# A graph-attention kernel: edges found in column groups, empty rows by a matmul, eleven batches

## The reference

```python
h = max(layernorm(x), 0);  x = x + L0(h, adj, W, a);  h = max(layernorm(x), 0);  return x + L1(h, adj)

# L0: attention with 4 heads of 32
Wh = (h @ W).reshape(N, 4, 32)
e = s_src[:, None, :] + s_dst[None, :, :]              # per head, from Wh and a
e = where(e >= 0, e, 0.2 * e);  e = where(adj[:, :, None] > 0, e, -9e15)
return elu(einsum('ijh,jhd->ihd', softmax(e, axis=1), Wh))    # a row without edges gets the mean of Wh
# L1: maximum over the neighbours
out = max over j with adj != 0 of x[j];  0 for rows without neighbours
```

## Time and profile before

| what | value |
| --- | --- |
| median of three runs | 566.72 us (566.58 to 567.52) |
| profiled execution, span | 568.4 us |
| PE, DVE, ACT, POOL busy | 64%, 73%, 53%, 64% |
| mean granted TensorE clock | 0.777 |
| DMA | 97.59 MB, 172 GB/s over the span |
| chain that ended last, by engine | POOL 14%, DMA 12%, issue 5%, PE 4% (the second stage's) |

### The profile page before, as it was taken

The page is one execution under the profiler, slowest core; times in us unless marked ns, Lnnn a source line. Parts: engine busy times, 40 slices in busy tenths (PEclk is TensorE's granted clock), DMA queues, the critical chain, the costliest instruction groups (busy, mean ns, idle before and its releaser), DMA issues. The chain is left out here.

```text
span 568.4 us, 9640 instructions
## 1 busy us (share of the span) xinstructions
PE 366.3 (64%) x2583; PEld 272.3 (48%) x2598; DVE 414.2 (73%) x1683; ACT 302.0 (53%) x747; POOL 364.5 (64%) x390
## 2 busy tenths in 40 slices
PE   1955367696768784984927373387766676667763
PEld 1723234363536463642917372155544565545553
DVE  7998896989968998798686768365656565565562
ACT  1988356465666766762020223465656565565661
POOL 5944377175777575676768521577777777777771
PEclk9979587797968797887665776567788778787687
DMA  8999868977989899761222100112222222332321
GB/s 265 390 282 425 349 229 296 329 277 258 369 316 342 338 342 359 288 225 40 52 52 39 44 28 28 46 53 56 57 62 58 64 62 67 69 66 68 72 69 38
DMA packets 36776, 97.59 MB, mean 172 GB/s; under 512 B 6896, under 2 KB 23536, under 8 KB 28528
## 3 DMA queue, kind: packets, MB, share of 16 engines
q1 hardware_dynamic: 18272, 71.51, 32.7%
q0 software_dynamic: 9984, 21.11, 15.8%
q10 hardware_dynamic: 8464, 4.33, 2.8%
HBM read 90.49 MB, written 6.42 MB: 171 GB/s over the span
## 5 line engine op out<-in xcount | busy, mean ns | idle before, releaser
L662 POOL DMA_INDIRECT G<-wh_table,idx x156 | 160.3, 1028 | 83.7 <-issue 45.0
L1284 POOL DMA_INDIRECT G<-h_table,idx x156 | 148.0, 949 | 52.4 <-issue 40.3
L682 ACT ACTIVATE adjb<-adjf 128x2048 bf16<-128x2048 int32 x64 | 121.7, 1902 | 48.2 <-PE psf L783 36.6
L1366 DVE TENSOR_TENSOR_SCAN S<-Fl,S,psf 128x128 f32<-128x128 f32 x117 | 56.1, 480 | 72.5 <-PE psf L1329 64.5
L1329 PE MATMUL psf<-identf,G 128*128 128x128 f32 x156 | 59.4, 380 | 61.8 <-DMA G<-h_table,idx 61.0
L1308 ACT COPY Sb<-psf 128x128 f32<-128x128 f32 x156 | 41.6, 267 | 81.3 <-PE psf L1335 80.3
L1344 PE MATMUL psf<-Sb,OL 128*128 128x128 f32 x312 | 79.8, 347 | 0.0
L782 PE MATMUL psf<-adjb,packw 128*128 128x512 bf16 x241 | 73.3, 457 | 9.1 <-ACT adjb L682 5.8
L1329 PEld LDWEIGHTS psf<-identf,G 128*128 128x128 f32 x156 | 26.2, 168 | 91.5 <-DMA G<-h_table,idx 89.2
L884 PE MATMUL psf<-E,OQ 128*128 128x64 f32 (+2 forms) x312 | 47.9, 326 | 26.6 <-DVE E L1124 26.6
L1294 ACT ACTIVATE dg<-identb,keep 128x128 bf16<-128x128 bf16 x156 | 63.0, 404 | 2.8 <-PEq L446 2.8
(11 more groups left out here) (142 smaller groups left out, 649.6 us busy)
## 6 DMA issues: line engine op xcount, KB each, us to landing
adjf<-in_adj_dram SPq DMA_DIRECT2D x64, 1024.0 KB, 9.2
G<-wh_table,idx POOLq DMA_INDIRECT x156
G<-h_table,idx POOLq DMA_INDIRECT x156, 2.5
wh_table<-OQ ACTq DMA_DIRECT2D x8, 272.0 KB, 4.8
xsf<-in_x_dram SPq DMA_DIRECT2D x4, 512.0 KB, 7.2
out_dram<-rows_out SPq DMA_DIRECT2D x32, 64.0 KB
h_table<-h1b ACTq DMA_DIRECT2D x2, 384.0 KB, 3.2
h_table<-h1b ACTq DMA_DIRECT2D x2, 256.0 KB, 2.3
```

The costliest lines, as they stand in the source:

```text
L662: pool.indirect_dma_start(G[:, plan.at[k] + b, :], None, wh_table, bass.IndirectOffsetOnAxis(ap=idx[:, n:n + 1], axis=0)).then_inc(gathere ...
L682: nc.scalar.activation(adjb[:, t % 2, c:c + N // 2], adjt[:, m % NA, :], ACT.Copy, accum_out=rc[:, t, m % 2:m % 2 + 1]).then_inc(adj_bf, 1)
L1284: pool.indirect_dma_start(G1[:, n % NG, :], None, h1_table, bass.IndirectOffsetOnAxis(ap=idx[:, n:n + 1], axis=0)).then_inc(found[n % NG], 16)
L1366: V.tensor_tensor_scan(S[:, n % 5, :], Fl[:, n % 3, :], ps[:, 1 + n % 2, 0:P], start, ALU.mult, ALU.max).then_inc(scan_done, 1)
```

## The change

From tile 4 on a row's K edges are no longer the K largest of all its candidates. The columns are in 2 to 4 groups (word c belongs to group c mod GR), and each group gets its own 8 slots: K = 8*GR. Such a unit is `flat`: no choice among words is made, and one MAX8 over the 64 candidates of a group gives its edges. Since a group's slots may be partly empty, `extract` also writes how many slots each earlier group left over, and `edges` turns an edge's place in the row into a slot with one compare and one max for each further group. Rows without neighbours get the mean of Wh (and 1 in the denominator) by a matmul of a diagonal `dnone`, made by ACT, into the sum of PE. The elu is computed as max(h, 0) + (min(exp h, 1) - 1), with exp straight from h. The cuts of the batches change, which makes eleven.

```diff
     def unit(t):
         b = blocks.get(t, 5 if t < 10 else 4 if t < 18 else 3)
-        return (t, 0, 1, 24 if t < 4 else 16, 8 if t < 4 else 4, b)
+        K, GR = (24, 8) if t < 4 else (32, 4) if t < 6 else (24, 3) if t < 12 else (16, 2)
+        return (t, 0, 1, K, GR, b)
-    cuts = [1, 2, 4, 7, 11, 16, 22, 28, tiles]
+    cuts = [1, 2, 4, 6, 9, 12, 17, 23, 29, tiles]
...
+def flat(unit):
+    return unit[2] == 1 and unit[3] == 8 * unit[4]
...
+    def steps(self, k):
+        u = self.batches[min(k, self.nb - 1)][0]
+        return u[4] - 1 if flat(u) else 0
+    def wide(self, k):
+        return self.batches[min(k, self.nb - 1)][0][3] + 7 + self.steps(k)
...
-        TAKE = [2, 2, 3, 3, 3, 4, 5, 5]
+        TAKE = [2, 2, 3, 2, 3, 3, 3, 5, 5]
         TAKE += [T - 1 - sum(TAKE)]
...
# scalar
-                    act.wait_ge(elu_in, f)
-                    nc.scalar.activation(ex[:, 0:len(tl), :], mn[:, 0:len(tl), :], ACT.Exp).then_inc(elu_out, 1)
+                    act.wait_ge(hp_ready, f)
+                    nc.scalar.activation(ex[:, 0:len(tl), :], hp[:, 0:len(tl), :], ACT.Exp).then_inc(ex_ready, 1)
...
                 for j, t in enumerate(plan.tiles(k - 2)):
+                    if j == 0:
+                        act.wait_ge(none_ready, k - 2)
+                    if t >= 2:
+                        act.wait_ge(agg_done, t - 1)
+                    nc.scalar.activation(dnone[:, t % 2, :], ident[:, :], ACT.Copy, scale=none[:, t:t + 1]).then_inc(dnone_ready, 1)
                     act.wait_ge(agg_done, t + 1)
...
# tensor
                         last = nc.tensor.matmul(ps[:, 6 + t % 2, 0:D + H], OQ[:, b, :], G[:, b, 0:D + H],
-                                                start=(n == 0), stop=(n == len(blocks) - 1))
-                    last.then_inc(agg_done, 1)
+                                                start=(n == 0), stop=False)
+                    if t == 0:
+                        pe.wait_ge(mean_ready, 2)
+                    pe.wait_ge(dnone_ready, t + 1)
+                    nc.tensor.matmul(ps[:, 6 + t % 2, 0:D + H], dnone[:, t % 2, :], mwh[:, :], start=False, stop=True).then_inc(agg_done, 1)
...
# vector, extract
                     for u in range(nu):
-                        n = mark(V.max(Xk[:, u, 8 * q:8 * q + 8], cnd[:, u * K * BITS:(u + 1) * K * BITS]))
-                    if q < K // 8 - 1:
+                        c0, c1 = (u * K * BITS, (u + 1) * K * BITS) if not steps else ((u * K + 8 * q) * BITS, (u * K + 8 * q + 8) * BITS)
+                        n = mark(V.max(Xk[:, u, 8 * q:8 * q + 8], cnd[:, c0:c1]))
+                    if q < K // 8 - 1 and not steps:
...
+                if steps:
+                    cg = part[:, 0:nu * GR].rearrange("p (u g) -> p u g", u=nu)
+                    yield from apart(V.tensor_reduce(cg, vk.rearrange("p u (g m) -> p u g m", m=8), AX, ALU.add))
+                    for i in range(1, GR):
...
# vector, edges
+                    yield from apart(V.tensor_tensor(pos, sel[:, :, K + 7:K + 7 + steps], spread(kq[:, bl], S, steps), ALU.add))
+                    for i in range(steps):
+                        n = mark(V.scalar_tensor_tensor(out=pos[:, :, i], in0=pos[:, :, i], scalar=8.0 * (i + 1), in1=pos[:, :, i],
+                                                        op0=ALU.is_ge, op1=ALU.mult))
...
+                    for i in range(steps):
+                        yield from apart(V.tensor_tensor(slot_q[:, 0:S], slot, pos[:, :, i], ALU.max))
...
# vector, finish and finish_rest
-                yield from apart(V.tensor_reduce(none[:, g], rc[:, g, :], AX, ALU.add))
-                yield from apart(V.tensor_scalar(none[:, g], none[:, g], 0.0, None, ALU.is_equal))
...
-                yield from apart(V.tensor_scalar(den[:, 0:nt, :], ag[:, 0:nt, D:D + H], 0.5, None, ALU.max))
...
-                    n = mark(V.scalar_tensor_tensor(out=hp[:, j, :], in0=mwh[:, :], scalar=none[:, t:t + 1], in1=hp[:, j, :],
-                                                    op0=ALU.mult, op1=ALU.add))
...
-                V.tensor_scalar(mn[:, 0:nt, :], hp[:, 0:nt, :], 0.0, None, ALU.min).then_inc(elu_in, 1)
+                yield from apart(V.scalar_tensor_tensor(out=xs[:, g, :].rearrange("p t d -> p (t d)"), in0=hp[:, 0:nt, :].rearrange("p t d -> p (t d)"), scalar=0.0,
+                                                        in1=xs[:, g, :].rearrange("p t d -> p (t d)"), op0=ALU.max, op1=ALU.add))
...
-                yield from apart(V.scalar_tensor_tensor(out=flat(hp[:, 0:nt, :]), in0=flat(hp[:, 0:nt, :]), scalar=0.0, in1=flat(ex[:, 0:nt, :]),
-                                            op0=ALU.max, op1=ALU.add))
-                yield from apart(V.scalar_tensor_tensor(out=flat(xs[:, g, :]), in0=flat(hp[:, 0:nt, :]), scalar=-1.0, in1=flat(xs[:, g, :]),
-                                            op0=ALU.add, op1=ALU.add))
+                yield from apart(V.tensor_scalar(line(ex[:, 0:nt, :]), line(ex[:, 0:nt, :]), 1.0, -1.0, ALU.min, ALU.add))
+                yield from apart(V.tensor_tensor(line(xs[:, g, :]), line(ex[:, 0:nt, :]), line(xs[:, g, :]), ALU.add))
```

More of the change, by code:

```diff
@@ L452, in edge_attention @@
         U = max(len(b) for b in plan.batches)
-        XW = max(len(b) * (b[0][3] + MW) for b in plan.batches)
+        XW = max(len(b) * plan.wide(k) for k, b in enumerate(plan.batches))
         SK = max(sum(u[5] for u in b) * b[0][3] for b in plan.batches)
@@ L485, in edge_attention @@
         some = sbl("some", [P, U])
+        part = sbl("part", [P, max(len(b) * b[0][4] for b in plan.batches)])
+        place = sbl("place", [P, max(plan.size[k] * plan.steps(k) for k in range(plan.nb))])
+        slot_q = sbl("slot_q", [P, SIZE])
         ends = sbl("ends", [P, 2, U])
@@ L515, in edge_attention @@
         bias = sbl("bias", [P, T])
[L516 removed]
+        wx = OQ[:, 12:14, :].rearrange("p a b -> p (a b)")[:, 0:WX]
         abc = OQ[:, 8:10, :].rearrange("p a b -> p (a b)")
@@ L829, in _ @@
             for k in range(NBT + 2):
-                K = plan.batches[min(k, NBT - 1)][0][3]
+                K, W_ = plan.batches[min(k, NBT - 1)][0][3], plan.wide(k)
                 if k < NBT:
@@ L857, in _ @@
                             for part in range(3):
-                                last = nc.tensor.matmul(ps[:, 2, o * (K + MW):(o + 1) * (K + MW)], Rm[:, plan.at[k] + o, :],
-                                                        Xb[:, part, u * (K + MW):(u + 1) * (K + MW)],
+                                last = nc.tensor.matmul(ps[:, 2, o * W_:(o + 1) * W_], Rm[:, plan.at[k] + o, :],
+                                                        Xb[:, part, u * W_:(u + 1) * W_],
                                                         start=(part == 0), stop=(part == 2))
@@ L942, in _ @@
             V.tensor_reduce(wx[:, D + H:D + 2 * H], wa[:, :, 0, :], AX, ALU.add).then_inc(wx_ready, 1)
+            V.memset(mwh[:, D:D + H], 1.0).then_inc(mean_ready, 1)
             for c in range(4):
@@ L968, in take_words @@
                     dve.wait_ge(packed, t + 1)
-                    words = ps[:, t % 2, :].rearrange("p (m g f) -> p f g m", g=GR, f=F)
                     for g in range(GR):
-                        last = V.max(wd[:, at + g * 8:at + g * 8 + 8], words[:, r, g, :])
+                        last = V.max(wd[:, at + g * 8:at + g * 8 + 8], ps[:, t % 2, r + g * F:C:GR * F])
                         if g < GR - 1:
@@ L1030, in rows_of_edges @@
                 nu, K = len(batch), batch[0][3]
-                W_ = nu * (K + MW)
+                W_ = nu * plan.wide(k)
                 Xk = X[:, k % 2, 0:W_].rearrange("p (u w) -> p u w", u=nu)
@@ L1088, in edges @@
                 dve.wait_ge(sel_done, k + 1)
-                sel = ps[:, 2, 0:S * (K + MW)].rearrange("p (b w) -> p b w", b=S)
+                sel = ps[:, 2, 0:S * plan.wide(k)].rearrange("p (b w) -> p b w", b=S)
                 n = mark(V.tensor_copy(meta[:, bl, :], sel[:, :, K:K + 3]))
                 mark(V.tensor_copy(sq[:, at, :], sel[:, :, K + 3:K + 7]))
+                steps = plan.steps(k)
                 yield
@@ L1127, in maxima @@
             def maxima(k):
+                tl = plan.tiles(k)
+                if tl:
+                    g = slice(tl[0], tl[-1] + 1)
+                    yield from apart(V.tensor_reduce(none[:, g], rc[:, g, :], AX, ALU.add))
+                    V.tensor_scalar(none[:, g], none[:, g], 0.0, None, ALU.is_equal).then_inc(none_ready, 1)
                 batch = plan.batches[k]
```

55 lines of the change are left out of this document (33 added, 22 removed).

## The result

The changed kernel took 582.76 us (median of four runs, 580.53 to 585.50) where the kernel before took 567.12 on the same chips: the ratio is 1.0249, with a 95% interval of 1.0215 to 1.0283. By the ratio it is slower by 14 us; the two medians lie 15.6 us apart. The forecast was 578.8, a ratio of 1.0213.

A forecast was written before the change was run, and what follows sets the result against it. From 229 us on, POOL's gathers plus hand-over were taken as the kernel's clock. `edge_max` starting 12.1 us later, at 373.1, and lasting an unchanged 207.4 gave a span of 580.5; less 1.7, 578.8 us, range 564 to 588.

The forecast's parts named there:

- the last step: Whole kernel, span to time: the span of 568.4 lay 1.7 us above the runs' median, so 580.5 became 578.8 us.
- The second stage unchanged: `edge_max`: its 156 gathers, their order and its code stay as they are, so it takes 207.4 us again.
- DVE's savings hidden: First stage: DVE is relieved by some 20 us net, and little of it lies on the path.
- One batch more: First stage, batches 4 to 10 instead of 4 to 9: the same 106 gathers, but six hand-overs for five.
- The gathers' times: POOL, first gathers of batches 5 to 10: 161.7, 186.6, 214.3, 248.0, 281.7 and about 314 us.
- PE's part between an E2 and L1080: PE's blocks at 0.234 us, 2.0 a pack, 0.4 for row counts: 8.8 us for batch 5, 9.3 for batch 6.
- The hand-over: POOL between batches: rstd, ACT's h1b, OQ and exponentials, then multiplications, delay the next gather; 8.35 us before, none of it DVE.
- Rival A: First stage paced by PE and DVE, not the gathers' loop: `edge_max` starts at 362 or 355, the latter 561 us; chance 0.17.
- The matmul: Aggregation, PE and ACT: the matmul with its activation adds 0.35 us a tile, bounds 0.23 to 0.6; 4.2 for two six-tile aggregations.
- B: Iterations 7 and 8: the adjacency loads can't follow with five tiles taken in each; price 3 to 8, 584 us; chance 0.12.
- C: POOL's gathers: if DVE holds POOL up, relief shortens 97 gathers by 0.08 each, 7.8 us: 571 us; chance 0.08.
- D: Search: a row with over 8 edges in one column group would force the many times slower `general_path`; excluded for this seed.

## Why the prediction was right, and where not

*Sign and size.* Right: slower was given 0.78, and the measured 582.76 lies in the range. The forecast was 4 us low, and only 0.9 of them lie in the sum: it gave a span of 580.5, and the profiled one is 581.4. The other 3.1 come from the last step. The prediction took 1.7 us off the span, because the span of 568.4 lay above the median of the runs before. But in every run listed here, and so in the profiled one after (583.04 us for 581.4), the time is 1.5 to 2.0 us longer than the span; the profiled execution before was a long one. That the span came out so well is in part luck: the exponentials of the last hand-over came 1.0 us late, the stretch to `edge_max` was 0.6 longer, and the second stage 0.8 shorter. The steps:

*The second stage unchanged*: 207.4 predicted, 206.6 measured.

*DVE's savings hidden*: right, and shown three times. The new cuts alone give nearly the same first gathers with the long search, the new search on the same eleven batches without the matmul is no faster, and ten batches with search and matmul give nothing. The estimate of DVE's net relief (some 20 us) was right too: 19.6 by the page. It went into L1080's waits: 35.1 us, where the kernel before has 4.7, the batches alone give 16.8, and batches and search 26.8. I expected 2 to 5 us for each; they were 5.94, 6.39, 3.72, 1.56, 6.16 and 11.32, the last because batch 10 has only three tiles to search while PE has 19 blocks of batch 8 to turn into rows and 20 of batch 7 to sum, most of it at the lower clock.

*One batch more*: right, and the largest term: 11.8 us by the cuts alone, 12.0 from ten to eleven, 13.4 from eleven to twelve (9.9, 12.0 and 10.9 by the ratios).

*The gathers' times*: batches 5 to 10 were predicted at 161.7, 186.6, 214.3, 248.0, 281.7 and about 314, and came at 163.38, 190.00, 217.06, 250.40, 284.19 and 314.98. POOL's idle before batch 5 was to be 8.7 and was 9.05. The mis-sized term is PE's part between an E2 and L1080: 8.8 and 9.3 us predicted for batches 5 and 6, 10.4 (141.34 to 151.74) and 10.9 (167.79 to 178.65) measured. I took a block's pair of L884 at 0.234 from a single row, at a granted clock of 1.00. In the first of these rounds the clock was 0.67 (141.4 to 146.5 us) and a pair took 0.35:

```profile
141.40 5.22 PE L905 MATMUL psf<-E,OQ 128*128 128x96 f32 x30 [1.82 <-DVE E L1178]
```

In the second it was 0.65 from 167.8 to 172.2 us. So the term was mis-sized by PE's clock: the sum priced the blocks of these rounds at the upper level.

From batch 7 on, the steps of 33.7 and 33.7 us were predicted, and 33.3 and 33.8 measured.

*The hand-over*: 8.1 us from the last gather of batch 8 (it ends at 276.09) to the first of batch 9 (284.19), where the earlier trace rows had 8.35, again with ACT in its middle. But the step by which, from 229 us on, this loop "is the clock of the kernel" fails. Taking ACT's h1b out of the hand-over moved the gathers and not the time, on either kernel. Rival A had the right second loop (PE and DVE) but made it too short: it had E2 of batch 9 end at some 305, and it ended at 317.2, and at 313.9 with the exponentials first. Its other price was also mis-summed, since three groups of 36 matmuls at 0.117 for 0.22 us would give 11 us and not 7; the lower clock stayed in the tail (0.50 in L905 at 317 and at 340 us). The mark of that second loop in the profile after is the 0.93 us of waiting for idx at 314.98. In the sum this did no harm, since both loops are about equally long and both were carried along to batch 7.

*The matmul*: 0.35 us a tile predicted with bounds of 0.23 and 0.6; 0.46 measured (1.15 less 0.69). The reason to take a value near the low end, that the activation overlaps the tile's own blocks, was wrong: ACT issues it after a copy for which it has waited for PE. In two groups of six tiles this makes 5.5 us for the 4.2 of the sum (an estimate; from the first to the last copy the two groups take 4.8 us longer than before). From the last exponential that POOL waited for ahead of the last gathers to `edge_max`, 62.8 was predicted and 63.4 measured.

*Rivals.* B: ACT waited 2.01 and 1.26 us for adjf from 237 to 243 us, but h1b at 245.12 then still waited 0.23 for POOL, so this cost next to nothing. C: the 106 gathers took 112.1 us with 30.5 of issue, 1.35 us each where they took 1.33:

```profile
L677 POOL DMA_INDIRECT G<-wh_table,idx x106 | 112.1, 1057 | 50.7 <-issue 30.5 <-DVE idx L1167 20.2
```

They did not get shorter though DVE was relieved by 20 us. The rule of the Trainium skill ("SBUF — State Buffer", section "SBUF: two separate sides"), by which POOL's descriptor writing is locked out while DVE is in a two-port mode, thus priced nothing here: the operations that the change removes were not what lengthened the gathers. No run here shows which were. D didn't occur.

*Open.* Moving the exponentials or offsets forward lengthened the stretch from the last batch's first gather to `edge_max` (59.8 us after, 61.6 with the exponentials first, 61.4 with both, and 62.3 for 60.5 on the kernel before); what in the tail takes it back was not found. A version with nine batches was not run, so whether one batch fewer would gain is open.

## What to carry to other kernels

In a pipeline written out by hand over engines that work in order, a further iteration has a price (here 10 to 13 us) though the work stays the same, because a round that passes from engine to engine hardly shrinks with its batch. A cheaper step inside pays only if it stands in the loop that closes last; before cutting work on the busiest engine, follow one whole round from a product to the same product of the next batch, over all engines. Where two loops are about equally long, an edit to one moves waits and no time, and an early wait on an in-order engine delays all that is queued behind it. Work moved to an engine for which the relieved one already waits can be a loss, the more so if it adds a hand-over for each tile (here some 2 us, within the noise). And a time is forecast from times: a span and a median of other executions don't give the offset between the two.

## What the runs showed of the hardware

No two indirect gathers of 128 rows started closer than 1.24 us in the first stage of any run (0.94 and 0.30 of issue), beside `adj`'s loads of some 300 GB/s or without them. The handing to and fro between PE and ACT for one tile, a pair of fp32 matmuls of 128x132 (0.49 us in most rows of the tail), a copy (0.27) and an activation of 128x128 (0.40), closed in 1.15 us in ten of the twelve steps of the tail and in 1.76 in the other two; in the 1.15, ACT spent 0.58 waiting. With the activation out of the circle it was 0.90 in eight of these twelve steps. PE's fp32 matmuls of 128x64 took 0.117 us each at a granted clock of 1.00 (40 in 4.68) and 0.22 at 0.50 (38 in 8.37). MAX8 over 64 columns took 0.135 us of the engine (7.8 us for 58), as the 0.142 of the earlier trace rows let expect.
